# A four-layer graph kernel on one core: refinement from new candidates with three row classes, layer norms by the statistics instruction, and two banks per product in the projections

## What is computed

```python
x = layernorm(x + L0(x, adj, h0, y))          # adj * (y @ y.T), rows divided by their sum, times x
x = layernorm(x + L1(x, adj, ...))            # below; ends in a layer norm of its own
x = layernorm(x + L2(x, adj, ...))            # masked attention with four heads
x = layernorm(x + L3(x, adj, ...))            # masked attention with one head, then a gated update

def L1(X, S, ...):                            # two steps of this
    q = X @ W1.T @ W2.T ; k = X @ W3.T
    probs = softmax(q @ k.T)                  # 5000 x 5000
    # of each row the largest entries are kept until their sum reaches 0.9 ("nucleus"),
    # the row is divided by what is kept, and A @ X goes into the next step
    # beside it R @ X, with R = (S + I) divided by its row sums ("diffusion")
```

## Time and profile before

| | |
|---|---|
| median of 3 runs | 6264.59 us (6263.4 to 6265.18) |
| the profiled execution | 6271.09 us |
| its span, first to last instruction | 6269.3 us |
| VectorE busy | 5090.3 us (81%) |
| TensorE busy (matmul) | 4393.9 us (70%) |
| ScalarE busy | 2200.1 us (35%) |
| GpSimd busy | 291.1 us (5%) |
| mean granted TensorE clock | 0.861 |

### The profile page before, as it was taken

How to read it: one execution, slowest core, us unless ns; L and a number is a source line. 1 busy time by engine, 2 the same in 40 slices (tenths; PEclk the granted TensorE clock), 3 DMA queues, 4 the chain that set the end, 5 groups by cost and what they waited for, 6 DMA issues and landing times. The chain is left out here.

```text
span 6269.3 us, 78468 instructions
## 1 busy us (share of the span) xinstructions
PE 4393.9 (70%) x27812; PEld 3146.2 (50%) x27812; DVE 5090.3 (81%) x12501; ACT 2200.1 (35%) x3353; POOL 291.1 (5%) x170
## 2 busy tenths in 40 slices
PE   6997688888779546263588778445278888837982
PEld 2443277777669545263477677445122222217982
DVE  5887388888628888998999999993679999975865
ACT  2332477777521111111245444232232221215542
POOL 0000000000030000000000000000002022110000
PEclk9998699999899778686799888777699999968996
DMA  7552000000057323041122222102033333314840
GB/s 198 201 202 98 17 2 2 2 2 2 1 157 227 110 82 112 26 139 53 47 74 79 76 69 69 35 2 34 18 112 106 111 109 108 105 29 187 298 173 17
DMA packets 183473, 546.63 MB, mean 87 GB/s; under 512 B 24603, under 2 KB 66702, under 8 KB 182902
## 3 DMA queue, kind: packets, MB, share of 16 engines
q1 hardware_dynamic: 177846, 536.71, 26.2%
q0 software_dynamic: 5120, 3.97, 0.3%
HBM read 528.97 MB, written 11.56 MB: 86 GB/s over the span
## 5 line engine op out<-in xcount | busy, mean ns | idle before, releaser
L680 PE MATMUL ps<-ident,arena 125*125 125x125 f32 x3200 | 539.4, 302 | 1030.1 <-DVEq L1189 1030.1
L680 PEld LDWEIGHTS ps<-ident,arena 125*125 125x125 f32 x3200 | 468.5, 214 | 1071.6 <-DVEq L1189 1071.6
L1491 DVE SCALAR_TENSOR_TENSOR arena<-arena,pair 125x1000 f32<-125x1000 f32 x800 | 939.2, 1252 | 70.7 <-ACT arena L1454 70.7
L794 ACT ACTIVATE turned<-ps 125x500 f32<-125x500 f32 x800 | 465.4, 585 | 1438.5 <-PE ps L680 1438.1
L688 PE MATMUL ps<-arena,turned 125*125 125x129 f32 x6400 | 917.6, 291 | 6.0 <-ACT turned L794 6.0
L1509 PE MATMUL ps<-arena 125*64 125x500 f32 x3200 | 764.0, 601 | 193.4 <-DVE arena L1491 193.4
L688 PEld LDWEIGHTS ps<-arena,turned 125*125 125x125 f32 x6400 | 843.8, 203 | 18.2 <-ACT turned L794 12.0
L712 PE MATMUL ps<-arena 125*125 125x129 f32 x6400 | 733.4, 275 | 24.5 <-ACT arena L805 17.4
L712 PEld LDWEIGHTS ps<-arena 125*125 125x125 f32 x6400 | 718.0, 188 | 59.6 <-issue 26.7
L1509 PEld LDWEIGHTS ps<-arena 125*64 125x64 f32 x3200 | 198.0, 137 | 756.4 <-DVE arena L1491 525.2
L1139 DVE SCALAR_TENSOR_TENSOR arena<-arena,wt 125x5000 f32<-125x5000 f32 x80 | 434.1, 5427 | 110.5 <-issue 110.5
(11 more groups left out here) (349 smaller groups left out, 5840.3 us busy)
## 6 DMA issues: line engine op xcount, KB each, us to landing
arena<-in_adj_tiles SPq DMA_DIRECT2D x400, 500.0 KB, 4.5
arena<-in_adj_wide SPq DMA_DIRECT2D x400, 500.0 KB, 4.4
arena<-in_adj_wide SPq DMA_DIRECT2D x100, 1000.0 KB, 4.5
x_saved<-arena SPq DMA_DIRECT2D x2, 2240.0 KB
arena<-x_saved SPq DMA_DIRECT2D x2, 2240.0 KB
arena<-att_saved SPq DMA_DIRECT2D x1, 2257.5 KB
arena<-in_x SPq DMA_DIRECT2D x1, 2240.0 KB
arena<-in_h SPq DMA_DIRECT2D x1, 2240.0 KB
```

Of the source, the lines that this page charges most:

```text
L680: mm = pe.transpose(banks_turn[:, g % 2, c * P:(c + 1) * P], work[b % depth][:, j:j + P], ident[0:P, 0:P])
L794: a.activation(turned[:, g % 2, :], banks_turn[:, g % 2, :], ACT.Copy)\
L1491: v.scalar_tensor_tensor(out=weight(m).rearrange("p (g w) -> p g w", g=2), in0=rows(ERB + h * N + r * PASS, PASS).rearrange("p (g w) -> p ...
```

## The change

1. In `refine` the numbers of bisections are arguments. The first refinement of a block makes none on whole rows and six on the new candidates; later ones make three and four as before.
2. Rows under `FAINT` = 0.35 of the mean squared query become a class of their own in front of the others, and `SPREADS` changes.
3. `layer_norm` takes mean and variance from `bn_stats`, one instruction for each of the 40 blocks, and applies them with one two-scalar instruction for each block. In layer 1 the statistics of a group are taken inside `mix_in`.
4. `transposed` uses four banks, and ScalarE and VectorE copy the groups in turn.
5. Both projections use two banks for each product and two buffers for the half query; TensorE makes the query product of group g - 1 behind the first products of group g.

The diff, cut to its core:

```diff
+FIRST_BISECTIONS = 6
+FAINT = 0.35
-SPREADS = (5, 3, [8, 8, 6, 6, 4, 0, 6, 6] + [1] * 28 + [0] * 4)
+SPREADS = (5, 3, [10, 10, 8, 4, 0, 6, 6, 5] + [1] * 23 + [0] * 9)
...
+        def halves_of(v, y, lo=0, hi=NB):
+            for b in range(lo, hi):
+                v.bn_stats(norm_parts[:, b, :], y[:, b, :])
+
+        def layer_norm(v, y, stat, s_var, s_std, n, known=False):
             mean, var = stat[:, 0:NB], stat[:, NB:2 * NB]
-            v.tensor_reduce(mean, y, AX.X, ALU.add)
+            if not known:
+                halves_of(v, y)
             v.drain()
-            v.tensor_scalar(mean, mean, 1.0 / F, None, ALU.mult)
+            part = lambda k: norm_parts[:, :, k:k + 1]
+            even, odd = part(1), part(4)
+            v.tensor_tensor(mean.unsqueeze(2), even, odd, ALU.add)
+            v.tensor_tensor(var.unsqueeze(2), part(2), part(5), ALU.add)
+            v.tensor_tensor(odd, odd, even, ALU.subtract)
             v.drain()
-            v.tensor_tensor(y, y, per_row(mean), ALU.subtract)
+            v.tensor_scalar(mean, mean, 0.5, None, ALU.mult)
+            v.tensor_tensor(even, odd, odd, ALU.mult)
+            v.tensor_scalar(var, var, 1.0 / F, LN_EPS, ALU.mult, ALU.add)
             v.drain()
-            v.tensor_tensor(sq, y, y, ALU.mult)
-            v.drain()
-            v.tensor_reduce(var, sq, AX.X, ALU.add)
-            v.drain()
-            v.tensor_scalar(var, var, 1.0 / F, LN_EPS, ALU.mult, ALU.add)
+            v.scalar_tensor_tensor(out=var.unsqueeze(2), in0=even, scalar=0.25, in1=var.unsqueeze(2),
+                                   op0=ALU.mult, op1=ALU.add)
             v.drain().then_inc(s_var, 1)
...
-            v.tensor_tensor(y, y, per_row(var), ALU.mult)
+            for b in range(NB):
+                v.tensor_scalar(y[:, b, :], y[:, b, :], mean[:, b:b + 1], var[:, b:b + 1], ALU.subtract, ALU.mult)
...
@@ transposed
-                        if g >= 2:
-                            pe.wait_ge(s_emptied, past + g - 1)
+                        if g >= 4:
+                            pe.wait_ge(s_copied_by[g % 2], past + g // 2 - 1)
...
+                @block.vector
+                def _(v):
+                    for g in range(1, NG, 2):
+                        v.wait_ge(s_turned_for[1], past + g // 2 + 1)
+                        v.tensor_copy(rows(dst + g * GW, GW, F), bank(g)).then_inc(s_copied_by[1], 1)
...
@@ keys_and_queries
+                    def second(g):
+                        pe.wait_ge(s_half, g + 1)
+                        if g >= 2:
+                            pe.wait_ge(s_query, g - 1)
+                        pe.matmul(bank_query[g % 2], wt[0:ATT, 128:192], half_q[g % 2], start=True, stop=True)
...
-                        if g:
-                            pe.wait_ge(s_v, 3 * g)
-                        pe.matmul(ps[0:ATT, 0, 0:GW], wt[0:F, 64:128], xs, start=True, stop=True)
-                        pe.matmul(ps[0:ATT, 1, 0:GW], wt[0:F, 0:64], xs, start=True, stop=True)
-                        pe.wait_ge(s_v, 3 * g + 2)
-                        pe.matmul(ps[0:ATT, 2, 0:GW], wt[0:ATT, 128:192], half_q, start=True, stop=True)
+                        if g >= 2:
+                            pe.wait_ge(s_key, g - 1)
+                        pe.matmul(bank_key[g % 2], wt[0:F, 64:128], xs, start=True, stop=True)
+                        if g >= 2:
+                            pe.wait_ge(s_half, g - 1)
+                        pe.matmul(bank_half[g % 2], wt[0:F, 0:64], xs, start=True, stop=True)
+                        if g:
+                            second(g - 1)
...
@@ keys_and_arranged_queries: the same order, and the places of three classes
-                    v.tensor_scalar(light, mine, limit, None, ALU.is_lt)
+                    v.tensor_scalar(flat_rows, mine, limit, None, ALU.is_lt)
+                    v.tensor_scalar(faint_rows, mine, limit_faint, None, ALU.is_lt)
...
@@ refine and step
-                    def refine(w, cand):
-                        for _ in range(BISECTIONS):
+                    def refine(w, cand, whole, among):
+                        for _ in range(whole):
                             bisect(w, dump, goal)
...
-                        for _ in range(CANDIDATE_BISECTIONS):
+                        for _ in range(among):
                             bisect(cand, windows, rest)
...
-                            refine(w, cand)
+                            refine(w, cand, 0, FIRST_BISECTIONS)
                             second = worst()
                             with v.If(second > 2):
-                                refine(w, cand)
+                                refine(w, cand, BISECTIONS, CANDIDATE_BISECTIONS)
...
@@ mix_in
+                        v.wait_ge(s_a, g + 1)
+                        halves_of(v, nodes(out_at, FA)[:, :, 0:F], g * GC, (g + 1) * GC)
```

More of the change, by code:

```diff
@@ L134, in gnn_kernel @@
         s_emptied = ctx.enter_context(nc.semaphore("bank_emptied"))
-        banks = {"used": 0}
+        s_turned_for = [ctx.enter_context(nc.semaphore(f"turned_for_{who}")) for who in ("scalar", "vector")]
+        s_copied_by = [ctx.enter_context(nc.semaphore(f"copied_by_{who}")) for who in ("scalar", "vector")]
+        banks = {"used": 0, "copied": 0}
         stat = cols[0:P, 0:2 * NB]
@@ L323, in _ @@
                     prepare(v)
[L324 removed]
+                    layer_norm(v, y, stat, s_var, s_std, 1)
                     v.memset(nodes(target, FA)[:, :, F:FA], 1.0)
@@ L400, in keys_and_queries @@
         def keys_and_queries(name):
-            with nc.semaphore(name + "_p") as s_p, nc.semaphore(name + "_v") as s_v, \
-                    nc.semaphore(name + "_q") as s_q, nc.Block() as block:
-                half_q = rows(SCR, GW, ATT)
+            with nc.semaphore(name + "_first") as s_first, nc.semaphore(name + "_key") as s_key, \
+                    nc.semaphore(name + "_half") as s_half, nc.semaphore(name + "_second") as s_second, \
+                    nc.semaphore(name + "_query") as s_query, nc.Block() as block:
+                half_q = [rows(SCR + k * GW, GW, ATT) for k in range(2)]
+                bank_key = [ps[0:ATT, k, 0:GW] for k in (0, 1)]
+                bank_half = [ps[0:ATT, k, 0:GW] for k in (2, 3)]
+                bank_query = [ps[0:ATT, k, 0:GW] for k in (4, 5)]
@@ L458, in _, with second @@
                 def _(pe):
+                    def second(g):
+                        pe.wait_ge(s_half, g + 1)
+                        if g >= 2:
+                            pe.wait_ge(s_own, g - 1)
+                        for c in range(GC):
+                            mm = pe.matmul(ps[0:P, 3 + g % 2, c * ATT:(c + 1) * ATT], half_q[g % 2][:, c * P:(c + 1) * P],
+                                           wt[0:ATT, 128:192], start=True, stop=True)
+                        mm.then_inc(s_second, 1)
                     for g in range(NG):
```

124 lines of the change are left out of this document (73 added, 51 removed).

## The result

The changed kernel takes 6173.35 us, the median of 4 runs (6170.96 to 6177.93), against 6264.89 us for the kernel before: a ratio of 0.9853, 95% interval 0.9841 to 0.9865. It is faster, as forecast, and inside the range (6070 to 6205), but 32 us above the forecast of 6141. The two profiled spans are 6269.3 and 6176.2 us: 93.1 us less, where the sum said 123 less. So 30 us of the expected gain have to be found.

What follows compares the result with a forecast made beforehand. VectorE was taken to bound the second nucleus step; in the first projection TensorE and ScalarE wait for each other. Terms 7 - 26.7 + 1.3 - 52 - 35 - 7 - 11 = -123 us gave 6141 us, range 6070 to 6205.

Steps and rivals of the forecast that it cites:

- Refinement: Second nucleus step: 11 short and 5 long refinements, so the new order of bisections only pays for itself, +7 us.
- Ties: Second nucleus step: two rows that caused separate tie passes now share block 6, so one pass goes, -26.7 us.
- Places of three classes: Before the nucleus step: about seven more small VectorE instructions on the path, +1.3 us (0.5 to 3).
- SPREADS: Second nucleus step: the rearranged diffusions stay hidden beside the steps, costed at nothing; at most 11 us might show.
- Layer norms: Four calls take 20.0 instead of 29.0 us each, the fifth saves 16 us: together -52 us (-16 to -87).
- some 10 us higher: Layer norms: the skill's fixed term, about 150 cycles per instruction, would raise the estimated sum by this much.
- Projections: First projection 29 instead of 64 us at full clock, -35 us; second with TensorE full, -7 us (0 to -8).
- rival (e): First projection stays at half clock: +26 us, total 6167 us; chance 0.07.
- Nothing to wait for: First projection: three products per group follow each other without waiting, 2.67 us per group instead of 6.4.
- Transposes: Nine transposing stages: two copying engines, four groups at 0.87 and six at 0.49 us, -11 us (0 to -20).
- (b): Second nucleus step: one more refinement or a new tie pass, total 6205 or 6168 us; chance 0.14.
- (d): The small instructions cost their upper bounds: +36 us, total 6177 us; chance 0.08.

Runs made afterwards that it cites:

- the third experiment: Changed kernel with the old first refinement (three whole-row bisections, four on candidates), keeping three classes and new SPREADS: 6085.16 us, ratio 0.9715.
- the two kernels by block: Changed kernel with first-refinement bisections set per block and the old refinement in the first nucleus step; new SPREADS 5939.89 us, old SPREADS 5940.62 us.
- the one-bank kernel: Changed kernel with one PSUM bank per product instead of two in the first projection, plus the waits this needs: 6174.10 us.
- the longer bodies: Changed kernel with the old refinement in the first nucleus step's branch bodies, which no block enters: 6170.38 us.

## Why the prediction was right, and where it was not

**Refinement, +7 forecast.** The counts were right in every block: 3 in block 0, 2 in blocks 1, 5 and 7, 1 in seven others; six bisections on candidates took 2317.30 - 2304.20 = 13.1 us, 2.18 each. The size was off in one step: the sum of 11 short and 5 long refinements counted the refinements but not the way out. A third refinement leads through nine idle loop turns, 1.3 us each. Of the 16.6 us missing in the second nucleus step, 13.2 are longer pauses in front of `keep` over the steps 0 to 39, before and after:

```profile
DVE arena L1139 <- issue: 57.6, 40, 6.0
```

```profile
DVE arena L1209 <- issue: 70.8, 40, 12.0
```

The loop of step 0 accounts for 6.0 of them: 12.0 us, where the kernel before already paused 6.0. Steps 3, 6 and 33 add 1.8, 2.7 and 3.2 us (now 5.5, 6.5 and 4.5 us). Each of these three holds two transfers of instructions, where the pauses of 3.5 us hold one; but step 2 of the third experiment has one of 5.4 us with a single transfer, so the count of transfers isn't the whole of it. Of the last 3.4 us, 2.3 lie in front of the first instruction of step 24 (6.2 us instead of 3.9, two transfers instead of one). These pauses I have from the trace alone; no run isolated them.

**Ties, -26.7.** Step 36 keeps its pass, step 6 has the one of the former steps 5 and 6. Right: fewer refinements and one pass less together gave 90.4 us where 90.2 were worked out.

**Places of three classes, +1.3.** From the sum over the squares to the first memset of the next stage it was 1762.89 - 1756.80 = 6.1 us, and is 1723.14 - 1715.74 = 7.4 us: right.

**SPREADS, 0.** Right, as far as neighbours show it: the two kernels by block take 5939.89 and 5940.62 us, and in the changed kernel VectorE waits for no exponentials in steps 0 to 5. The changed kernel itself wasn't run with the old list.

**Layer norms, -52.** 7.83 us for forty `bn_stats`, 0.194 us apart to the last digit of the estimate, and 10.36 instead of 10.1 us for the apply; 20.7 instead of 20.0 us. The fifth, with its statistics in `mix_in`, ends 13.8 us after the last addition instead of 29.3: -15.5 where -16 was said. The value from the nearest row, MAX8, fitted; it too reads a short row and writes a few numbers, but that this is why it fitted isn't shown. The Trainium skill ("VectorE: DVE Perf Modes", section on the TRN2 errata), cited in the prediction, warned rightly of a cost per instruction. Its measured fixed term of about 150 cycles is that of one instruction's duration, and there the trace is near it: a `bn_stats` lasts 0.276 us, 0.139 more than the 0.137 us of 128 elements at 1.07 ns. But the next one starts before it has ended, so that in a row only 0.057 us of fixed time is paid, as in MAX8. The prediction's "some 10 us higher" took the term of a duration for that of a distance, and it is too small by its own terms: the 160 `bn_stats` of four calls times the difference between the two terms of the Trainium skill are some 15 us, an estimate from that page.

**Projections, -35 and -7.** From its first product to the next stage's first instruction the first went from 64.2 to 28.7 us, the second from 3.57 to 2.83 us per group. The full clock was granted throughout; the half clock of rival (e) didn't come, with one bank per product or with two. "Nothing to wait for" holds within 0.13 us (2.80 instead of 2.67 us per group), but not because of the two banks that the title names, as the one-bank kernel showed.

**Transposes, -11.** The sum is right (-11.3), its parts are not: the slow stretch lasted six groups in the second stage and was absent in the short one (4.46 us for ten groups). The two errors cancel.

**The step that failed**, though the time lies in the range, is one that the prediction took without a word: that a stage whose executed instructions stay as they are keeps its time. "I cost all this at nothing" was said of the SPREADS, where a cover could be named; of the first nucleus step nothing was said, and it cost 11.2 us, of which 9.7 came back with the longer bodies. The diff shortens code there that doesn't run, and the pause with a transfer of instructions then comes every fourth time instead of every sixth. With the 16.6 us of the second nucleus step this is 28 of the 30 us.

**The rivals.** None of them came. (b), one more refinement or tie pass, gives 6168 or 6205 us and by its total alone would have looked right; the counts exclude it. (d), upper bounds of the small instructions, gives 6177 and is excluded by the 20.7 us of a layer norm. A total that fits a rival proves nothing while the counts can be read.

The order also answers a question that the prediction had left aside: "the new order of bisections pays for itself and no more" weighed the short refinement against the order of before. Against the order that the same change brings in, where the old refinement needs a second turn in one block only, it loses: 4 x 63.5 - 11 x 16.7 = +70 us by the same prices, and 83 us measured in the second nucleus step. The prices for that stood in the earlier trace rows before the result was known.

## What to carry to other kernels

Price the parts of a change against each other, not only the whole against the kernel before: here one part gave back all of the 86 us that its neighbour had won, and by its total the change looked sound. A loop that retries work until it suffices should be sized for each block by what that block needs, and its way out counted as part of the price. When a stage that nothing touches changes its time, compare the pauses one by one before looking for contention: a fixed period in steps, with a transfer of instructions inside each long pause, points to the place of the code.

## What was not expected of the hardware

- In front of `keep`, behind a branch of VectorE's program, the idle time in the first nucleus step was 0.9 to 1.8 us or 3.1 to 3.8, the longer always with an 8192-byte transfer of instructions inside it. Which of the two it was changed with the length of code that is never entered: 3 to 11 of 40 equal steps had the long one, 927.5 to 947.8 us for the same work.
- A turn of a loop that loads a register, compares and does nothing took 1.3 us ((11.98 - 1.63) / 8), with no transfer of instructions beside it.
- `bn_stats` on 128 fp32 elements starts every 0.194 us and lasts 0.276, a two-scalar `tensor_scalar` on 128 elements starts every 0.257 us.
